# Routed experts: rows turned by VectorE in 32x32 blocks, down product copied by ScalarE

## What is computed

```python
scores = sigmoid(xf @ gate_w.T)
top_scores, top_idx = top_k(scores, 2)
top_scores = top_scores / (top_scores.sum(-1) + 1e-20) * 2.5
# the rows of each expert are collected in buf[E=64]
h = silu(buf @ w1[e]) * (buf @ w3[e])          # w1, w3: [512, 256]
y = h @ w2[e]                                  # w2: [256, 512]
routed = sum over the 2 choices of top_scores * y
shared = silu(xf @ sw1) * (xf @ sw3) @ sw2
out = x + shared + routed
```

## Time and profile before

| | us |
|---|---|
| median of 3 runs | 2392.26 |
| lowest, highest | 2389.78, 2392.93 |
| profiled execution, span | 2392.9 |
| item loop in it | about 1823 to 2236 |

### The profile page before, as it was taken

How to read it: one execution, slowest core, us unless ns; L and a number is a source line. 1 busy time by engine, 2 the same in 40 slices (tenths; PEclk the granted TensorE clock), 3 DMA queues, 4 the chain that set the end, 5 groups by cost and what they waited for, 6 DMA issues and landing times. The chain is left out here.

```text
span 2392.9 us, 35675 instructions
## 1 busy us (share of the span) xinstructions
PE 2009.4 (84%) x8716; PEld 1279.8 (53%) x8716; DVE 1416.6 (59%) x3001; ACT 1020.9 (43%) x3220; POOL 1027.6 (43%) x1051
## 2 busy tenths in 40 slices
PE   5957888888887625259999999897899999999998
PEld 4745666666665313124433444354346888888544
DVE  6646888988888762476666656577852222222343
ACT  2325777777776603465666656344001111111000
POOL 1037777777772404257777777300001111111331
PEclk9978999999999657779999999999999999999999
DMA  5547888888883734777777777785316999999652
GB/s 147 124 151 240 243 246 237 244 239 241 244 235 94 287 107 99 192 249 223 224 224 225 223 223 225 246 283 180 123 53 214 361 368 365 366 366 364 226 191 88
DMA packets 276214, 537.31 MB, mean 225 GB/s; under 512 B 43507, under 2 KB 121947, under 8 KB 275859
## 3 DMA queue, kind: packets, MB, share of 16 engines
q0 software_dynamic: 80544, 261.97, 37.4%
q1 hardware_dynamic: 177043, 240.65, 29.5%
q10 hardware_dynamic: 18464, 32.84, 4.0%
HBM read 449.56 MB, written 86.57 MB: 224 GB/s over the span
## 5 line engine op out<-in xcount | busy, mean ns | idle before, releaser
L852 POOL DMA_INDIRECT g_G<-tab,src_of_item x440 | 445.6, 1013 | 178.6 <-issue 109.1
L917 PE MATMUL g_psA<-g_G,g_oh 128*128 128x261 f32 x1760 | 444.1, 399 | 61.7 <-DVE g_G L1067 48.7
L1222 PE MATMUL g_psA<-g_G,g_oh 128*128 x832 | 387.5, 608 | 76.2 <-SPq L1178 69.0
L1162 POOL DMA_INDIRECT g_G<-tab,src_of_tile x392 | 371.0, 946 | 165.7 <-issue 82.0
L974 ACT ACTIVATE g_G<-g_G 128x64 f32<-128x64 f32 x1760 | 425.1, 336 | 0.0
L1265 DVE TENSOR_TENSOR acc<-acc,g_psA 128x512 f32 x416 | 285.7, 687 | 186.1 <-PE g_psA L1222 145.4
L917 PEld LDWEIGHTS g_psA<-g_G,g_oh 128*128 128x128 f32 x1760 | 327.0, 194 | 125.5 <-DVE g_G L1067 62.4
L1222 PEld LDWEIGHTS g_psA<-g_G,g_oh 128*128 128x128 f32 x832 | 146.4, 190 | 294.4 <-issue 293.1
L2441 PE MATMUL mo_bank<-mo_xT,mo_w 128*128 128x128 f32 x2304 | 269.1, 275 | 0.3 <-ACT mo_xT L2478 0.3
L2344 POOL DMA_INDIRECT mo_g<-tab,mo_slot x72 | 68.1, 946 | 456.9 <-PE mo_bank L2431 325.0
L2441 PEld LDWEIGHTS mo_bank<-mo_xT,mo_w 128*128 128x128 f32 x2304 | 263.0, 192 | 1.0 <-ACT mo_xT L2478 0.5
(11 more groups left out here) (425 smaller groups left out, 2532.4 us busy)
## 6 DMA issues: line engine op xcount, KB each, us to landing
mo_w<-in_L_ffn_w SPq DMA_DIRECT2D x216, 512.0 KB, 8.5
ys<-mo_y ACTq DMA_DIRECT2D x72, 256.0 KB, 5.6
g_ot<-reld SPq DMA_DIRECT2D x27, 512.0 KB, 5.8
ys<-sg_zeros SPq DMA_DIRECT2D x24, 512.0 KB, 4.5
g_G<-tab,src_of_item POOLq DMA_INDIRECT x440
g_pen<-pend SPq DMA_DIRECT2D x216, 32.0 KB
tab<-fi_row SPq DMA_DIRECT2D x25, 261.0 KB, 2.7
xmid<-at_x SPq DMA_DIRECT2D x25, 256.0 KB, 5.1
```

The source lines that it names most:

```text
L852: q.indirect_dma_start(G[:, j % RING, :], None, tab0, bass.IndirectOffsetOnAxis(K.src[:, j:j + 1], 0)).then_inc(gs[g % 3], 16)
L917: ins = tens.matmul(psA[u][:, f, 0:HW], oh[:, n % OR, h, :], G[:, r + h, f * HW:(f + 1) * HW], start=(h == 0), stop=(h == SUP - 1))
L1162: g.indirect_dma_start(G[:, (j + 1) % MR, :], None, table, bass.IndirectOffsetOnAxis(K.src1[:, j:j + 1], 0)).then_inc(got[j % MR], 16)
L1222: tens.matmul(psA[n % MB][:], oh[:, n % MO, :], G[:, ds(tile1 % MR, 1), :].rearrange("p o d -> p (o d)"), start=True, stop=True).then_inc( ...
```

## The change

In the item loop, TensorE's four transposes per item, the PSUM bank `eX`, ScalarE's copy of it and the semaphore `cop` go. In their place VectorE turns the rows of `g` directly into `xT`, both in SBUF. VectorE's transpose works on blocks of 32x32, so the 128x128 tiles are turned in sixteen instructions per item. Instruction (r, c) reads the 32 partitions from 32r on, of which it takes 32 columns from 32c on in each of the four 128-column tiles (128 values per partition), and writes the 32 partitions of `xT` from 32c on, columns 32r to 32r+31 of each tile. r is the outer loop and c the inner one. They stand at the head of VectorE's step, for item n, behind waits for the gathered rows and for the up product of n-2, whose `xT` buffer they overwrite; the last one signals `turned`. TensorE waits for `turned` ahead of the up product of n-1.

VectorE's copy of the down product to `y` moves to ScalarE, between the sigmoid of n-1 and the store of n-3. ScalarE's and VectorE's steps both keep their other work.

```diff
-        eX, eH, eY = psA, psB, psR
+        eH, eY = psB, psR
+        QD = P // 4
@@ TensorE
-                u = q % 2
-                if n_ok(n, q, 0):
-                    t.wait_ge(got[q], k * 16 + 16)
-                    wait(t, cop, n - 1)
-                    for kt in range(KT):
-                        ins = tens.transpose(eX[u][:, kt * P:(kt + 1) * P], g[:, q, kt * P:(kt + 1) * P], K.ident[:])
-                    ins.then_inc(turned, 1)
                 m, km, qm = prev(n, k, q, 1)
                 um = qm % 2
                 if n_ok(n, q, 1):
-                    t.wait_ge(cop, m + 1)
+                    t.wait_ge(turned, m + 1)
@@ ScalarE
-                if n_ok(n, q, 0):
-                    u = q % 2
-                    c_.wait_ge(turned, n + 1)
-                    wait(c_, up, n - 1)
-                    nc.scalar.activation(xT[:, u], eX[u][:].rearrange("p (k t) -> p k t", k=KT), ACT.Copy).then_inc(cop, 1)
                 m, km, qm = prev(n, k, q, 1)
                 um = qm % 2
                 if n_ok(n, q, 1):
                     c_.wait_ge(up, m + 1)

                     nc.scalar.activation(sg[:, um, :], eH[um][:, 0:F1], ACT.Sigmoid).then_inc(sgd, 1)
+                m, km, qm = prev(n, k, q, 2)
+                if n_ok(n, q, 2):
+                    c_.wait_ge(yd, m + 1)
+                    wait(c_, st[qm], km * 16)
+                    nc.scalar.activation(y[:, qm, :], eY[qm % 2][:], ACT.Copy).then_inc(yc, 1)
@@ VectorE
+            def turn_rows(q):
+                for r in range(4):
+                    for c in range(4):
+                        ins = vv.transpose(xT[c * QD:(c + 1) * QD, q % 2, :, r * QD:(r + 1) * QD],
+                                           g[r * QD:(r + 1) * QD, q, :].rearrange("p (k c e) -> p k c e", k=KT, c=4)[:, :, c, :])
+                return ins
+
             def step(n, k, q):
+                if n_ok(n, q, 0):
+                    v.wait_ge(got[q], k * 16 + 16)
+                    wait(v, up, n - 1)
+                    turn_rows(q).then_inc(turned, 1)
                 m, km, qm = prev(n, k, q, 1)
                 um = qm % 2
                 if n_ok(n, q, 1):
@@
-                m, km, qm = prev(n, k, q, 2)
-                um = qm % 2
-                if n_ok(n, q, 2):
-                    v.wait_ge(yd, m + 1)
-                    wait(v, st[qm], km * 16)
-                    vv.tensor_copy(y[:, qm, :], eY[um][:]).then_inc(yc, 1)
-            run(v, 2, step)
+            run(v, 1, step)
```

More of the change, by code:

```diff
@@ L2241, in phase_moe @@
         turned = p.sem("turned")
-        cop = p.sem("cop")
         up = p.sem("up")
```

## The result

The changed kernel takes 2411.7 us (median of 4, 2406.0 to 2415.9) where the kernel before takes 2392.6 in the same comparison: a ratio of 1.009, 95% interval 1.0072 to 1.0108. It is slower by some 19 us, the way that was forecast; the forecast was +44.5 us.

A forecast was written before the change was run, and what follows sets the result against it. TensorE bounded the loop at 5.73 us per item; VectorE was to become the bound at 16p + 0.95 = 6.29 us. The change, 1152p - 340.2 us with p = 0.334, gave +44.5 us, 2437 us; range 2376 to 2485.

The forecast's parts named there:

- the pieces run end to end: VectorE's sixteen transposes per item: each starts only when the last is done, 0.334 us apart; chance 74%.
- TensorE's share: Item loop: without its transposes (0.44 us) TensorE has 5.29 us of work per item instead of 5.73.
- the move of the copy: Down product's copy, VectorE to ScalarE: VectorE loses about 0.69 us, ScalarE gains 0.60 us; cost nothing.
- the queues: GpSimd's and SyncE's queues: weight loads wait as before, gathers are released by VectorE's last piece; cost nothing.
- the distance between pieces: VectorE, one piece's start to the next (p): taken as 0.334 us, bounds 0.21 and 0.367; ten nanoseconds are 11.5 us.
- rest of VectorE's item: VectorE's item besides the pieces: 0.45 + 0.42 + 2 x 0.04, making the item 16p + 0.95 us.
- the end-to-end case: The forecast itself, 74%: p from 0.294 (no gap, 2391 us) to 0.367 us (2475 us).
- The clock: TensorE's granted clock, with PE idling one microsecond per item: costed at nothing.
- PE at about 84%: Sign in the item loop: PE about 84% busy, its up product waiting on VectorE's transpose once per item.
- Pieces overlap, but the DMA engines can't follow: Item loop: 5.29 us per item asks for 396 GB/s; at 380 GB/s an item takes 5.52 us, 2381 us; chance 5%.
- The first rival: VectorE's pieces overlap, p = 0.21 us, PE stays the bound with 5.29 us per item: 2365 us; chance 14%.
- Two passes: VectorE's piece needs two passes for four-byte values, p = 0.46 us: +190 us, 2582 us; chance 7%.

The follow-up runs named there:

- e3: Changed kernel with the copy of the down product back on VectorE: 2448.6 us, ratio 1.0246 to the kernel before.
- e6: Changed kernel with ScalarE's sigmoid replaced by SiLU, so that one of VectorE's two multiplications goes: 2380.9 us, ratio 0.9971 to the kernel before.
- e1: Changed kernel with all sixteen pieces at full height (128 partitions), rows turned only in part, run for time alone: 2376.8 us, ratio 0.9955 to the kernel before.
- e2: Changed kernel with the loops over r and c exchanged, so the written quarter stays for four pieces: 2412.3 us, ratio 1.0099 to the kernel before.
- e5: Changed kernel with every piece cut in two, 32 pieces of 64 values per partition: 2479.8 us (one run).
- e7: Changed kernel, but TensorE turns the even items and VectorE the odd ones: 2375.1 us, ratio 0.9939 to the kernel before.
- e4: Kernel before with only the copy of the down product moved to ScalarE, transposes left on TensorE: 2390.8 us, ratio 1.0000.
- e8: Even/odd split of turns between TensorE and VectorE, plus features dealt to partitions as 4p + k (4 KB weight runs): 2403.9 us, ratio 1.0068 to the kernel before.
- e9: Changed kernel, but item 0 alone is turned by TensorE and copied by ScalarE: 2407.6 us, ratio 1.0074 to the kernel before.
- e10: Changed kernel, but TensorE turns every fourth item and VectorE the three others: 2381.0 us, ratio 0.9963 to the kernel before.

## Why the prediction was wrong

*That VectorE becomes the bound and the kernel slower: right.* The waits of the changed kernel show it, and e3 and e6 move the time with VectorE's work.

*That the pieces run end to end, and because the quarter changes: right.* It stood there as a reason without a row. e1, e2 and e5 are the rows. They show that a change of quarter holds a piece back; what goes on in the engine meanwhile (lanes that have to be empty) they don't show.

*TensorE's share, the move of the copy, the queues: right.* TensorE's two products take 3.57 + 1.72 = 5.29 us in e7, where it is the bound, e4 shows the copy at nothing, and GpSimd's gathers never delayed an item.

*The size: wrong, by one term above all, the distance between pieces.* The loop length was reckoned as 458.4 us and is 435.8:

| term of the sum | reckoned | measured | difference, us |
|---|---|---|---|
| start, items 0 and 1 turned | 32 x 0.334 = 10.7 | 10.1 | -0.6 |
| wait for the first up product | 0 | 1.9 | +1.9 |
| 16 pieces, 70 periods | 16 x 0.334 = 5.34 | 16 x 0.316 = 5.06 | -20.2 |
| rest of VectorE's item, 70 periods | 0.95 | 0.89 | -4.0 |
| end | 7.1 | 7.3 | +0.2 |

The period measured is (2248.72 - 1832.29) / 70 = 5.949 us. The step that failed is the piece. It was put at 294 ns plus a gap of 40 ns, and the gap came from neighbours that are tied by a semaphore. The pieces aren't: no wait stands between them, the engine holds them back by itself, and that gap is 14 ns. The duration was 8 ns too low (302). The two errors are of opposite sign and partly cancel. The 18 ns left on a piece are 20 us on the kernel, as the prediction's own slope says (11.5 us for each 10 ns). It named that sensitivity, but of the end-to-end case it took a gap that belongs to another kind of tie. The middle between no gap (0.294) and 40 ns (0.334), 0.314 us, would have given 1152 x 0.314 - 340.2 = +21.5, or 2414 us; no row of before pointed to it, so that would have been luck.

In the rest of the item the first piece was thought to start 0.04 us after the multiplication's end. It starts 0.08 before it (2022.95 + 0.42 against 2023.29): both begin at partition 0, so that piece isn't held. That alone would make 0.45 + 0.34 + 0.03 = 0.82 us; the idle time at each turn of the loop, every fourth item, adds some 0.08 to the mean. The clock was costed at nothing by a stage that runs steadily. In the loop that holds, 1.00 throughout; at its start TensorE stands still for 5.8 us, and the prediction didn't follow TensorE there. The first up product at 0.50 is behind the 1.9 us of the table's second row: with the 3.84 us that it took before it would have ended at 1829.2, ahead of the end of item 1's turn (1830.36).

*The signs.* "PE at about 84%" was read off distances and compared with a busy time that counts overlap: it showed 93%. GB/s were to fall to 333 and fell to 351 to 353, since the item is shorter than reckoned: 2.10 MB in 5.95 us are 352.

*The rivals.* "Pieces overlap, but the DMA engines can't follow" was worked out to within 4 us (e1: 2377 against 2381), and e1 suggests that it would have come about but for the quarters. The first rival, overlap with TensorE as the bound (2365 us), had the right distance for pieces whose quarters stay (0.21 against 0.195) and didn't come about in any run. "Two passes" is out.

The net of the loop, +21.9 us, and small differences ahead of it (-2.0) and behind it (+1.4) make the profiled span's +21.3; the medians say +19.1.

## What to carry to other kernels

Before work is moved to an idle engine, its item time there has to be compared with the bound it is to relieve, and with how many instructions it is made of: 16 x 0.316 + 0.89 = 5.95 us on VectorE replaced 0.44 us on TensorE, against a bound of 5.73. When the result hangs on the distance between short instructions, take that distance from neighbours of the same kind of tie (semaphore, none, other partitions), and state the time per ten nanoseconds. And a job that is too long for one engine may be shared: every second item on VectorE (e7) gave 0.6%, where all of them lost 0.9%.

## What the runs showed of the hardware

- VectorE's pieces with 128 values per partition: 0.195 us apart when read and written quarter stay (e1, 128 partitions high, 272 ns each), 0.316 when either changes (changed kernel and e2, 32 high, 302 ns each). With 64 values and 32 partitions (e5): 0.169 when both stay, 0.207 when one changes.
- A read with a step of four float32 values made a VectorE piece 98 ns longer (e8, 400 ns), and left TensorE's transposes nearly alone.
- In this loop's mix of transfers the DMA engines gave 375 to 378 GB/s at most, with weight loads landing in up to 11.6 us (e1); at 365 to 367 GB/s the loads landed in 8.5 us in one kernel and in 5.2 in another (before, e4). The Trainium skill, "DMA: Bandwidth & Descriptors", section "Specifications", lists 435 GB/s for the fabric, some 358 for one core's share of the memory and 368 as a derate; the runs lie a little above the last two and far below the first.
- TensorE's granted clock was 0.50 at the first up product after a standstill of 5.8 us, and again after gaps of 1.5 and 0.7 us in one execution (e9), but 1.00 after the same gaps in two others (e7, e10).
